# A feed-forward bias that enters through a 64-row matmul instead of a GpSimd addition

## The chip, the cores and the metric

The kernel runs on one NeuronCore of a Trainium2 chip. The time is that of one execution on the device, in microseconds (us); several executions are made and their median is what counts. The engines are called by the names of the profile: PE is TensorE (PEld its weight loads), DVE is VectorE, ACT is ScalarE, POOL is GpSimd and SP is SyncE.

## The reference

`x` has 4 sequences of 1024 tokens with 256 features (float32), `ctx` 154 tokens for each sequence. One block of gated cross attention and one gated feed-forward layer:

```
x = x + tanh(g_xattn) * attention(layernorm(x), ctx, mask, ...)   # 4 query heads of 64, one key/value head
h = gelu(layernorm(x) @ ternary(W1).T + b1)                       # 256 -> 1024
x = x + tanh(g_ffn) * (h @ ternary(W2).T + b2)                    # 1024 -> 256
```

`ternary(w)` replaces each weight by -1, 0 or 1 (round of `w` over its mean magnitude, clipped). The bias of the change is `b2`, a vector of 256 numbers that is added to every token's output.

## The kernel before, in words

The 4096 tokens are worked on as 8 groups (`NG = 8`) of 512 tokens, each group as 4 tiles (`NT = 4`) of 128 tokens. Every engine runs its own list of instructions, in an order that is written out by hand in a function `step(i, p, b)`; `i` is the number of the step, and one step does work of three groups: the attention of group `i`, the first feed-forward product, gelu and split (`ffn_in`, `gelu`, `split_h`) of group `i-1`, and the second feed-forward product `ffn_out` of group `i-2`. Steps 0 and 1 are written out, steps 2 to 5 come from a loop of two steps each, steps 6 and 7 and the two last ones (8 and 9, that have no attention) are written out again. Engines wait for each other through semaphores alone.

PE multiplies in float32r. Where the precision asks for it an operand is split into a high part (`_hi`, written by ACT as float32r) and the rest (`_lo`, written by DVE by subtraction), and both parts are multiplied. So `ffn_out(t)` (L1103) is 8 chunks times 2 parts = 16 matmuls of 128 contraction rows and 256 columns that add up in one PSUM bank. PSUM banks `ps_m` are two, taken in turn by `q1, q2, y0, q3, y1, y2, y3, att0, ...` (`M_ORDER`, L221); before a bank is written again, `bank_m` (L1008) waits until DVE has read what was in it two uses ago. DVE's `ffn_out(t)` (L785) takes the bank, multiplies by the gate and adds to the tile of `x1` (L796). `x1` holds the output of the attention part; its layer norm (`x1n`, ACT L519) is taken before anything else is added to it.

The bias: in the set-up DVE makes `b2_gated = tanh(g_ffn) * b2` (L725) in all 128 partitions. In each step from 1 to 8 POOL adds it to the four tiles of `x1` in one instruction (`add_b2`, L384 to L391) between its `normalise(0)` and `normalise(1)` (L402 to L408, that divide the softmax by its sum). It waits for `x1n_done`, so that the layer norm has read `x1` first, and DVE waits for `y_base` ahead of each L796.

In step order PE does (L1163 on): `q_T(0)`, `q(1)`, `q(2)`, `scores(0)`, `ffn_out(0)`, `q_T(1)`, `q(3)`, `ffn_out(1)`, `q_T(2)`, `x1_T(0)`, `scores(1)`, `ffn_out(2)`, `q_T(3)`, `x1_T(1)`, `scores(2)`, `ffn_out(3)`, `scores(3)`, `p_T(0)`, `tail_T(0)`, `ffn_in(0)`, `ffn_in(1)`, `p_T(1)`, and so on. `p_T` and the other transposes write `ps_t`, whose two banks come free when DVE has done its `lo_part` (L650). `products` (L925 to L929) is the helper in which most matmuls are recorded, as L928. In step 9 PE does the rest of `last_out` (L1123): its 16 matmuls for each tile are L1133, and two of the tiles start within step 8, between the pieces of `ffn_in`.

Of the kernel before, what the change touches and what calls it, by code (L numbers as in the profile page):

```python
# [7 lines left out]
F32 = mybir.dt.float32  # L8
F32R = mybir.dt.float32r
U8 = mybir.dt.uint8  # L10
ALU = mybir.AluOpType
# [17 lines left out]
def flamingo_block(nc, x, ctx_main, ctx_tail, mask, gates, rms_scale, wq, wk, wv, wo, w1t, b1, w2t, b2,  # L29
# [10 lines left out]
    NF = F // P  # L40
    TAIL = S - P
    TP = 32
    HP = H // 2
    CT = B + 1
    assert H * TP == P and B * TP == P and 2 * C == P and NG == 2 * B and KD == 2
# [4 lines left out]
    with ExitStack() as ctx:  # L50
# [26 lines left out]
        w_scale = sb("w_scale", [P, 2])  # L77
        w_thr = sb("w_thr", [P, 2, 2])
        b1_sb = sb("b1_sb", [P, NF])
        b2_gated = sb("b2_gated", [P, D])  # L80
        mask_u8 = sb("mask_u8", [P, B, S], U8)
        mask_bias = sb("mask_bias", [P, B, S])
        mask_now = sb("mask_now", [P, S])
# [85 lines left out]
        def psum(name):  # L169
# [9 lines left out]
        x_in = [sem("x_in0"), sem("x_in1")]  # L179
        out_done, last_out_done = [sem("out_done0"), sem("out_done1")], [sem("last_out_done0"), sem("last_out_done1")]  # L180

        const_set, ctx_zeroed, zeros_set, gate_set = (
            sem(n) for n in ("const_set", "ctx_zeroed", "zeros_set", "gate_set"))
        ctx_bn_done, ctx_stats, ctx_ms_done, ctx_rstd, ctx_normed, ctxT_filled, ctxT_copied = (
            sem(n) for n in ("ctx_bn_done", "ctx_stats", "ctx_ms_done", "ctx_rstd", "ctx_normed",
                             "ctxT_filled", "ctxT_copied"))
# [17 lines left out]
            sem(n) for n in ("bn1_done", "ln1_stats", "ln1_var", "ln1_rstd"))  # L204
        bn2_done, ln2_stats, ln2_var, ln2_rstd, ln2_shift, x1n_done = (
            sem(n) for n in ("bn2_done", "ln2_stats", "ln2_var", "ln2_rstd", "ln2_shift", "x1n_done"))
        q_roped, exp_done, inv_done, prob_done, y_base = (
            sem(n) for n in ("q_roped", "exp_done", "inv_done", "prob_done", "y_base"))


        def has(i):
# [129 lines left out]
        @block.gpsimd  # L341
        def _(pool):
            pool.memset(ctx_sb[:, B, :], 0.0).then_inc(ctx_zeroed, 1)
            pool.memset(neghalf[:], -0.5).then_inc(const_set, 1)
            pool.memset(ones_sb[:], 1.0).then_inc(const_set, 1)
            pool.dma_start(gate_raw[:, :], gates.partition_broadcast(P)).then_inc(gate_in, 16)
            pool.dma_start(mask_u8[:], mask.partition_broadcast(P)).then_inc(mask_in, 16)
            pool.dma_start(b2_raw, b2.partition_broadcast(P)).then_inc(b2_in, 16)

            pool.memset(prob_tail[:], 0.0).then_inc(zeros_set, 1)  # L350
            pool.memset(kk_hi[:].bitcast(F32), 0.0).then_inc(zeros_set, 1)
            pool.memset(kk_lo[:].bitcast(F32), 0.0).then_inc(zeros_set, 1)
            pool.memset(v_tail.bitcast(F32), 0.0).then_inc(zeros_set, 1)

            pool.wait_ge(ctx_stats, 1)
            pool.tensor_tensor(ctx_m2[:], ctx_mv[:, :, 0], ctx_mv[:, :, 0], ALU.mult).then_inc(ctx_ms_done, 1)
            pool.wait_ge(ctx_ms_done, 1)
            pool.tensor_tensor(ctx_ms[:], ctx_m2[:], ctx_mv[:, :, 1], ALU.add).then_inc(ctx_ms_done, 1)
            pool.wait_ge(ctx_ms_done, 2)
            pool.tensor_scalar(ctx_me[:], ctx_ms[:], RMS_EPS, None, ALU.add).then_inc(ctx_ms_done, 1)  # L360
            pool.wait_ge(ctx_ms_done, 3)
            pool.wait_ge(const_set, 1)
            pool.tensor_tensor(ctx_r[:], ctx_me[:], neghalf[:, 0:CT], ALU.pow).then_inc(ctx_rstd, 1)

            def rstd(ve, r, var_sem, rstd_sem, i):
                pool.wait_ge(var_sem, i + 1)
                pool.tensor_tensor(r[:], ve[:], neghalf[:, 0:NT], ALU.pow).then_inc(rstd_sem, 1)

            rstd(ve1, r1, ln1_var, ln1_rstd, 0)

            pool.wait_ge(wo_hi_set, 1)
            pool.tensor_tensor(wo_lo[:], wo_raw[:], wo_hi[:], ALU.subtract).then_inc(wo_set, 1)
            def rope_add(i, t):
                pool.wait_ge(m_read, m_use(i, f"q{t}") + 1)
                q = q_cos[t % 2][:].rearrange("p (h j c) -> p h j c", h=H, j=2)
                swapped = q_sin[t % 2][:].rearrange("p (h j c) -> p h j c", h=H, j=2)[:, :, ::-1, :]
                pool.tensor_tensor(q, q, swapped, ALU.add).then_inc(q_roped, 1)  # L377

            def step(i, p, b):
                att, nxt, f1, _ = has(i)  # L380

                first = isinstance(i, int) and i == 0

                def add_b2():  # L384

                    if f1:
                        pool.wait_ge(x1n_done, i * NT)
                        if isinstance(i, int) and i == 1:
                            pool.wait_ge(b2_set, 1)
                        b2s = b2_gated[:].rearrange("p (a d) -> p a d", a=1).to_broadcast([P, NT, D])  # L390
                        pool.tensor_tensor(x1[1 - p], x1[1 - p], b2s, ALU.add).then_inc(y_base, 1)  # L391

                def rstd2():
                    if f1:
                        rstd(ve2, r2, ln2_var, ln2_rstd, i - 1)

                if not att:
                    rstd2()
                    add_b2()
                    return  # L400

                def normalise(t):  # L402
                    pool.wait_ge(inv_done, i * NT + (t + 1))
                    inv = p_inv[:, t, :].rearrange("p (h a) -> p h a", a=1)
                    main, tail = prob[t][:, :, 0:P], prob[t][:, :, P:S]
                    pool.tensor_tensor(main, main, inv.to_broadcast([P, H, P]), ALU.mult)  # L406
                    pool.tensor_tensor(prob_tail[:, t, :, 0:TAIL], tail, inv.to_broadcast([P, H, TAIL]),
                                       ALU.mult).then_inc(prob_done, 1)  # L408

                rope_add(i, 1)  # L410
                rstd2()
                rope_add(i, 2)
                rope_add(i, 3)
                normalise(0)
                add_b2()
                normalise(1)
                if first:
                    w_low_piece(0)
                normalise(2)
                if first:  # L420
                    w_low_piece(1)
                if nxt:
                    rstd(ve1, r1, ln1_var, ln1_rstd, i + 1)
                normalise(3)
                if first:
                    for n in range(2, 2 * PIECES):
                        w_low_piece(n)
                if nxt:
                    rope_add(i + 1, 0)

            rope_add(0, 0)

            pool.wait_ge(v_set, 2)
            pool.wait_ge(zeros_set, 4)
            for h in range(H):
                pool.tensor_copy(v_tail[:, :, h, TP * h:TP * (h + 1)],
                                 v_T[:, B * P:].rearrange("p (b j) -> p b j", b=B)).then_inc(v_tail_set, 1)

            def w_low_piece(n):

                m, cols = n // PIECES, slice(n % PIECES * PIECE, (n % PIECES + 1) * PIECE)
                if n == 0:
                    pool.wait_ge(w_thr_set, 2)
                if n >= NL:
                    pool.wait_ge(w_set, n - NL + 1)
                pool.tensor_scalar(w_low[n % NL], w_raw[m][:, cols], w_thr[:, 1, m:m + 1], None,  # L446
                                   ALU.is_lt).then_inc(w_low_set, 1)

            loop(pool, step)
# [169 lines left out]
        def _(dve):  # L619
# [102 lines left out]
            dve.tensor_scalar(mask_bias[:], mask_u8[:], MASK_FILL, -MASK_FILL, ALU.mult, ALU.add).then_inc(mask_f_set, 1)  # L722
            dve.wait_ge(gate_set, 1)
            dve.wait_ge(b2_in, 16)
            dve.tensor_scalar(b2_gated[:], b2_raw, gate[:, 1:2], None, ALU.mult).then_inc(b2_set, 1)  # L725
            dve.wait_ge(mask_f_set, 1)

            def vw_lo_part(n):

# [22 lines left out]
            def step(i, p, b):  # L752
# [32 lines left out]
                def ffn_out(t):  # L785
# [3 lines left out]

                    n = m_use(i, f"y{t}")  # L790
                    dve.wait_ge(m_filled, n + 1)
                    dve.wait_ge(y_base, i - 1)
                    ys = x1[p][:, t, :]
                    last = isinstance(i, int) and i > NG
                    src = last_bank(t) if last else m_bank(i, f"y{t}")
# [128 lines left out]
        def _(pe):  # L924
# [83 lines left out]
            def bank_m(i, what):  # L1008
# [2 lines left out]
                    pe.wait_ge(m_read, n - 1)  # L1011
                return m_bank(i, what)[:, 0:D]

            def q(i, t):
                tile = slice(P * t, P * (t + 1))
                products(bank_m(i, f"q{t}"), [(a[:, k, tile], w[:, k, :]) for k in range(KD)
# [3 lines left out]
            def step(i, p, b):  # L1020
# [82 lines left out]
                def ffn_out(t):  # L1103
# [2 lines left out]
                        return  # L1106
                    w = w_tern[1][:].rearrange("p (c d) -> p c d", c=NF)
                    dst = bank_m(i, f"y{t}")
                    for c in range(NF):
                        if t == 0 and c in (0, NF - 2):  # L1110
                            pe.wait_ge(h_split, (i - 1) * NF - (2 if c == 0 else 0))
                        for a in (hT_hi, hT_lo):
                            m = pe.matmul(dst, a[:, c, P * t:P * (t + 1)], w[:, c, :],  # L1113
                                          start=(c == 0 and a is hT_hi), stop=(c == NF - 1 and a is hT_lo))
                    m.then_inc(m_filled, 1)

                def x_T(k):
# [5 lines left out]
                def last_out(t, chunks):  # L1123

                    w = w_tern[1][:].rearrange("p (c d) -> p c d", c=NF)
                    for c in chunks:
                        if c == 0 and t < 2:
                            dst = bank_m(NG + 1, f"y{t}")
                        else:
                            dst = last_bank(t)[:, 0:D]  # L1130
                        pe.wait_ge(h_split, (NG - 1) * NF + c + 1)
                        for a in (hT_hi, hT_lo):
                            m = pe.matmul(dst, a[:, c, P * t:P * (t + 1)], w[:, c, :],  # L1133
                                          start=(c == 0 and a is hT_hi), stop=(c == NF - 1 and a is hT_lo))
                        if c == NF - 1:
                            m.then_inc(m_filled, 1)

# [129 lines left out]
```

## Time and profile before

| | |
|---|---|
| median of 3 runs | 347.42 us (346.23 to 348.87) |
| the profiled execution | 346.31 us, of which the span from first to last instruction is 344.4 us |
| matmuls | 2175, PE busy 91% of the span |
| DVE, ACT, POOL busy | 74%, 68%, 37% |
| mean granted TensorE clock | 0.97 of 2.4 GHz, 1.00 between 117 and 289 us |
| one step of the loop, from a start of `ffn_out(1)` on PE to the next (151.10 to 185.98) | 34.9 us |
| L391, the addition on POOL | 8 times, 2.4 us each |

Busy shares are means over the whole span. A matmul's time in the profile runs from its start to the modelled end of its results, so in a full pipeline the next one starts well before: what a matmul takes of the engine is the distance between two starts.

### The profile page before, as it was taken

To read this page: it belongs to the slowest core of one execution; us is meant where nothing else is said; L and a number is where in the kernel's file an instruction comes from. 1 tells how busy PE (TensorE), PEld (TensorE's weight loads), DVE (VectorE), ACT (ScalarE), POOL (GpSimd) and SP (SyncE) were. 2 spreads that over 40 slices of the span, in tenths; PEclk is the share of its full clock that TensorE was granted. 3 is DMA by queue.
4 is the path that set the end of the run, shared out by engine and by line. 5 is a ranking of instruction groups with operands and counts; after the bars stand their busy time and mean duration, and the time that the engine had idled before them with its cause. 6 is when DMAs were issued, how large, how long until landed. Compare 5 with 4: busy or idle time off the path is not lost.

```text
span 344.4 us, 6831 instructions
## 1 busy us (share of the span) xinstructions
PE 311.7 (91%) x2175; PEld 285.4 (83%) x2175; DVE 256.4 (74%) x825; ACT 232.5 (68%) x595; POOL 127.0 (37%) x151
## 2 busy tenths in 40 slices
PE   8299649766699999999999999999999999999996
PEld 8297539655599988998899988998899889988976
DVE  0567884998559986988698869986998697858443
ACT  0144793337597579757975797579758985896492
POOL 8231237954510363036303540353136313630300
PEclk9769998998799999999999999999999999999999
DMA  6943000020000110011002100110011000100101
GB/s 127 284 129 122 2 0 2 0 64 1 0 2 0 64 47 17 0 63 48 17 0 61 46 15 0 61 46 15 0 64 46 18 0 2 47 17 2 46 16 63
DMA packets 12983, 13.35 MB, mean 39 GB/s; under 512 B 1781, under 2 KB 12397, under 8 KB 12957
## 3 DMA queue, kind: packets, MB, share of 16 engines
q1 hardware_dynamic: 11004, 11.52, 10.4%
q10 hardware_dynamic: 1824, 1.30, 1.5%
q0 software_dynamic: 128, 0.21, 0.8%
q8 instruction: 14, 0.23, 0.3%
q14 instruction: 13, 0.10, 0.1%
HBM read 8.83 MB, written 4.19 MB: 38 GB/s over the span
## 4 chain that ended last, share of the span: by engine, by line
PE 64%; DVE 21%; issue 4%; POOL 4%; ACT 3%; DMA 2%; SPq 0%; DVEq 0%; POOLq 0%
PE ps_m L928 18%; PE ps_h L928 17%; PE ps_m L1113 10%; PE ps_s L928 5%; PE ps_t L936 4%; PE ps_t L1062 3%; DVE s_neg L765 3%; DMA w_raw<-in_ctx_tail 2%; POOL hT_lo L446 2%; DVE s_neg L763 2%; DVE q_sin L708 2%; DVE s_min L769 1%; DVE q_cos L705 1%; DVE x1nT_lo L650 1%; DVE pT_lo L650 1%
## 5 line engine op out<-in xcount | busy, mean ns | idle before, releaser
L406 POOL TENSOR_TENSOR prob<-prob,p_inv 128x512 f32<-128x512 f32 x32 | 33.4, 1044 | 72.4 <-DVE p_inv L773 72.4
L377 POOL TENSOR_TENSOR q_cos<-q_cos,q_sin 128x256 f32<-128x256 f32 x32 | 23.5, 735 | 97.6 <-DVE q_sin L708 97.6
L928 PE MATMUL ps_h<-x1nT_hi,w_tern 128*128 128x512 f32 x128 | 55.0, 429 | 3.1 <-DVE vw_lo L732 2.6
L526 ACT ACTIVATE prob<-s_neg,s_min 128x154 f32<-128x154 f32 x128 | 52.5, 414 | 5.8 <-DVE s_min L769 4.9
L1113 PE MATMUL ps_m<-w_tern,hT_hi 128*128 128x256 f32 x224 | 55.3, 285 | 0.7 <-DVE x_both L796 0.2
L1113 PE MATMUL ps_m<-w_tern,hT_lo 128*128 128x256 f32 x224 | 54.7, 282 | 0.0
L928 PE MATMUL ps_h<-x1nT_lo,w_tern 128*128 128x512 f32 x128 | 51.3, 401 | 0.0
L824 DVE TENSOR_TENSOR hT_lo<-h_all,hT_hi 128x512 fp32r<-128x512 f32 x64 | 42.0, 691 | 8.8 <-ACT hT_hi L557 8.8
L557 ACT ACTIVATE h_all<-ps_h,b_sb 128x512 f32<-128x512 f32 x64 | 45.6, 712 | 3.2 <-PE ps_h L928 2.2
L928 PE MATMUL ps_m<-vw_hi,pT_hi 128*128 128x256 f32 (+1 forms) x160 | 46.7, 292 | 0.0
L557 ACT ACTIVATE hT_hi<-ps_h,b_sb 128x512 fp32r<-128x512 f32 x64 | 45.7, 714 | 0.0
L928 PE MATMUL ps_m<-vw_hi,pT_lo 128*128 128x256 f32 (+1 forms) x160 | 45.2, 283 | 0.0
L928 PE MATMUL ps_m<-vw_lo,pT_hi 128*128 128x256 f32 (+1 forms) x160 | 45.2, 282 | 0.0
L1113 PEld LDWEIGHTS ps_m<-w_tern,hT_hi 128*128 128x128 f32 x224 | 42.6, 190 | 1.9 <-DVE x_both L796 1.9
L476 ACT ACTIVATE qT_hi<-ps_t 128x256 fp32r<-128x256 f32 x32 | 12.2, 382 | 46.1 <-PE ps_t L1037 46.1
L1113 PEld LDWEIGHTS ps_m<-w_tern,hT_lo 128*128 128x128 f32 x224 | 42.7, 191 | 0.0
L650 DVE TENSOR_TENSOR pT_lo<-ps_t,pT_hi 128x512 fp32r<-128x512 f32 x64 | 29.4, 481 | 17.5 <-ACT pT_hi L476 16.9
L928 PEld LDWEIGHTS ps_h<-x1nT_hi,w_tern 128*128 128x128 f32 x128 | 24.6, 192 | 11.3 <-ACT hT_hi L557 4.6
L476 ACT ACTIVATE pT_hi<-ps_t 128x512 fp32r<-128x512 f32 x64 | 27.2, 451 | 8.6 <-PE ps_t L1062 8.5
L928 PEld LDWEIGHTS ps_m<-vw_lo,pT_hi 128*128 128x128 f32 x160 | 30.6, 191 | 0.3
L928 PEld LDWEIGHTS ps_m<-vw_hi,pT_hi 128*128 128x128 f32 x160 | 30.5, 191 | 0.4
L928 PEld LDWEIGHTS ps_m<-vw_hi,pT_lo 128*128 128x128 f32 x160 | 30.6, 191 | 0.0
(136 smaller groups left out, 802.4 us busy)
## 6 DMA issues: line engine op xcount, KB each, us to landing
x_sb<-in_x SPq DMA_DIRECT2D x8, 512.0 KB, 3.6
out_x<-x_both SPq DMA_DIRECT2D x8, 384.0 KB, 2.5
h_all<-in_w1t SPq DMA_DIRECT2D x1, 1024.0 KB, 13.7
w_raw<-in_w2t SPq DMA_DIRECT2D x1, 1024.0 KB, 5.4
out_x<-x_both SPq DMA_DIRECT2D x8, 128.0 KB, 1.7
w_raw<-in_ctx_main SPq DMA_DIRECT2D x1, 512.0 KB
wo_raw<-in_wo ACTq DMA_DIRECT2D x2, 256.0 KB, 10.2
x_both<-in_wq ACTq DMA_DIRECT2D x1, 256.0 KB, 10.7
```

The source lines that it names most:

```text
L377: pool.tensor_tensor(q, q, swapped, ALU.add).then_inc(q_roped, 1)
L406: pool.tensor_tensor(main, main, inv.to_broadcast([P, H, P]), ALU.mult)
L476: nc.scalar.activation(dst, src, ACT.Copy).then_inc(t_hi, 1)
L526: e = nc.scalar.activation(prob[t][:, h, :], s_neg[t % 2][:, h, :], ACT.Exp, bias=s_min[t % 2][:, h:h + 1], scale=-1.0, accum_out=p_sum[:, ...
L557: g = nc.scalar.activation(dst, ps_h[c % 2][:], ACT.Gelu, bias=b1_sb[:, c:c + 1])
L650: dve.tensor_tensor(dst, src, hi, ALU.subtract).then_inc(t_lo, 1)
L765: dve.tensor_tensor_reduce(s[:, h, :], ps_s[h // 2][:, S * (h % 2):S * (h % 2 + 1)], mask_now[:], 1.0, 3.4e38, ALU.add, ALU.min, least[:, ...
L824: dve.tensor_tensor(hT_lo[:, c, :], h_act[c % 4][:], hT_hi[:, c, :], ALU.subtract).then_inc(h_split, 1)
L928: m = pe.matmul(dst, lhs, rhs, start=(n == 0), stop=(n == len(pairs) - 1))
L936: m = pe.transpose(dst[:, P * t:P * (t + 1)], src[:, t, P * k:P * (k + 1)], ident_sb[:])
L1062: m = pe.transpose(t_bank(i, f"p{t}")[:, P * h:P * (h + 1)], prob[t][:, h, 0:P], ident_sb[:])
L1113: m = pe.matmul(dst, a[:, c, P * t:P * (t + 1)], w[:, c, :], start=(c == 0 and a is hT_hi), stop=(c == NF - 1 and a is hT_lo))
```

## The change

The bias enters as the first matmul of each output tile. A tile `b2_rows` holds, in partitions 0 to 31, `b2` rounded to float32r and, in partitions 32 to 63, what the rounding lost; `mean_rows` is filled with 1/32. One matmul of 64 contraction rows (`start_with_b2`) then puts `b2` into each row of the PSUM bank, and the 16 products add to it. The gate is applied by DVE's L796, as for the products. POOL's `add_b2`, its semaphore `y_base` and DVE's wait for that go; POOL sets `mean_rows` at the start; DVE's one multiplication L725 becomes a copy, a wait for the copy, and a subtraction over 32 partitions.

```diff
-        b2_gated = sb("b2_gated", [P, D])
+        b2_rows = sb("b2_rows", [P, D], F32R)
+        mean_rows = sb("mean_rows", [P, P], F32R)
...
+            pool.memset(mean_rows[:].bitcast(F32), 1.0 / ROWS).then_inc(mean_set, 1)
             pool.memset(prob_tail[:], 0.0).then_inc(zeros_set, 1)
...
-                def add_b2():
-
-                    if f1:
-                        pool.wait_ge(x1n_done, i * NT)
-                        if isinstance(i, int) and i == 1:
-                            pool.wait_ge(b2_set, 1)
-                        b2s = b2_gated[:].rearrange("p (a d) -> p a d", a=1).to_broadcast([P, NT, D])
-                        pool.tensor_tensor(x1[1 - p], x1[1 - p], b2s, ALU.add).then_inc(y_base, 1)
...
                 if not att:
                     rstd2()
-                    add_b2()
                     return
...
                 normalise(0)
-                add_b2()
                 normalise(1)
...
             dve.wait_ge(b2_in, 16)
-            dve.tensor_scalar(b2_gated[:], b2_raw, gate[:, 1:2], None, ALU.mult).then_inc(b2_set, 1)
+            dve.tensor_copy(b2_rows[:], b2_raw).then_inc(b2_hi_set, 1)
             dve.wait_ge(mask_f_set, 1)
+            dve.wait_ge(b2_hi_set, 1)
+            dve.tensor_tensor(b2_rows[ROWS:2 * ROWS], b2_raw[ROWS:2 * ROWS], b2_rows[ROWS:2 * ROWS],
+                              ALU.subtract).then_inc(b2_set, 1)
...
                     dve.wait_ge(m_filled, n + 1)
-                    dve.wait_ge(y_base, i - 1)
...
+            def start_with_b2(dst):
+
+                pe.matmul(dst, mean_rows[0:2 * ROWS, :], b2_rows[0:2 * ROWS, :], start=True, stop=False)
...
                     dst = bank_m(i, f"y{t}")
+                    if isinstance(i, int) and i == 2 and t == 0:
+                        pe.wait_ge(mean_set, 1)
+                        pe.wait_ge(b2_set, 1)
+                    start_with_b2(dst)
                     for c in range(NF):
...
                             m = pe.matmul(dst, a[:, c, P * t:P * (t + 1)], w[:, c, :],
-                                          start=(c == 0 and a is hT_hi), stop=(c == NF - 1 and a is hT_lo))
+                                          start=False, stop=(c == NF - 1 and a is hT_lo))
...
+                        if c == 0:
+                            start_with_b2(dst)
                         pe.wait_ge(h_split, (NG - 1) * NF + c + 1)
```

## Rows read from the trace of the kernel before

**Rows 1.** The page's busy times and shares of the span

```profile
PE 311.7 (91%) x2175; PEld 285.4 (83%) x2175; DVE 256.4 (74%) x825; ACT 232.5 (68%) x595; POOL 127.0 (37%) x151
```

**Rows 2.** L391 alone: ns min/median/max; the list of waiters is empty

```profile
L391 POOL TENSOR_TENSOR x_both<-x_both,b_gated x8: 2381/2415/2422, 84.7 to 322.4; 128x1024 f32<-128x1024 f32 x8
...
who waited for it (us, times):
```

**Rows 3.** The chain in order of time, one step: start us, us, what

```profile
151.10 2.18 PE ps_m L1113 x16
...
154.78 1.92 PE ps_m L1113 x16
...
158.25 0.32 DVE s_neg L763
...
160.92 0.76 issue
...
163.64 0.66 PE ps_t L1062 x4
```

**Rows 4.** Timeline of PE, its idle time and the last matmuls ahead of it

```profile
150.76 0.28 PE L928 MATMUL ps_m<-wq_hi,xT_lo 128*128 128x256 f32 x1
151.10 0.39 PE L1113 MATMUL ps_m<-w_tern,hT_hi 128*128 128x256 f32 x1
151.32 0.28 PE L1113 MATMUL ps_m<-w_tern,hT_lo 128*128 128x256 f32 x1
...
163.00 0.40 PE L928 MATMUL ps_h<-x1nT_lo,w_tern 128*128 128x512 f32 x1
163.64 0.66 PE L1062 MATMUL ps_t<-ident_sb,prob 128*128 128x128 f32 x4 [0.25 <-DVE pT_lo L650]
```

**Rows 5.** Timeline of POOL and DVE around one L391

```profile
158.33 2.42 POOL L391 TENSOR_TENSOR x_both<-x_both,b_gated 128x1024 f32<-128x1024 f32 x1
160.69 1.06 POOL L406 TENSOR_TENSOR prob<-prob,p_inv 128x512 f32<-128x512 f32 x1
...
156.76 0.17 DVE L773 RECIPROCAL p_inv<-p_sum 128x4 f32<-128x4 f32 x1
157.01 1.04 POOL L406 TENSOR_TENSOR prob<-prob,p_inv 128x512 f32<-128x512 f32 x1 [2.73 <-DVE p_inv L773]
...
160.41 0.17 DVE L773 RECIPROCAL p_inv<-p_sum 128x4 f32<-128x4 f32 x1
160.87 0.90 DVE L641 TENSOR_SCALAR ve<-mv 128x4 f32<-128x4 f32 x1
```

**Rows 6.** The chain at the end of the kernel

```profile
296.90 1.91 PE ps_m L1113 x16
...
317.41 5.74 PE ps_m L1113 x48
...
324.03 1.91 PE ps_m L1113 x16
...
329.42 0.48 PE ps_m L1133 x4
...
339.53 2.17 PE ps_t L1133 x18
```

**Rows 7.** Timeline of DVE in the set-up, and the PE work behind it

```profile
34.18 0.35 DVE L725 TENSOR_SCALAR b_gated<-x_both,gate 128x256 f32<-128x256 f32 x1
34.55 0.42 DVE L650 TENSOR_TENSOR qT_lo<-ps_t,qT_hi 128x256 fp32r<-128x256 f32 x1
...
35.68 0.23 DVE L866 COPY mask_now<-mask_bias 128x154 f32<-128x154 f32 x1
...
35.03 0.41 PE L928 MATMUL ps_s<-kk_hi,qT_hi 128*128 128x308 f32 x1 [0.89 <-DVE qT_lo L650]
```

**Rows 8.** Timeline of POOL at the start

```profile
1.02 0.20 POOL L345 MEMSET ones_sb<- 128x128 f32 x1
...
12.78 0.20 POOL L356 TENSOR_TENSOR ctx_m<-ctx_mv 128x5 f32<-128x5 f32 x1 [5.17 <-DVE ctx_mv L625]
```

More of the change, by code:

```diff
@@ L42, in flamingo_block @@
     TP = 32
+    ROWS = 32
     HP = H // 2
@@ L180, in flamingo_block @@
         out_done, last_out_done = [sem("out_done0"), sem("out_done1")], [sem("last_out_done0"), sem("last_out_done1")]
-        const_set, ctx_zeroed, zeros_set, gate_set = (
-            sem(n) for n in ("const_set", "ctx_zeroed", "zeros_set", "gate_set"))
+        const_set, ctx_zeroed, zeros_set, gate_set, mean_set, b2_hi_set = (
+            sem(n) for n in ("const_set", "ctx_zeroed", "zeros_set", "gate_set", "mean_set", "b2_hi_set"))
         ctx_bn_done, ctx_stats, ctx_ms_done, ctx_rstd, ctx_normed, ctxT_filled, ctxT_copied = (
@@ L206, in flamingo_block @@
             sem(n) for n in ("bn2_done", "ln2_stats", "ln2_var", "ln2_rstd", "ln2_shift", "x1n_done"))
-        q_roped, exp_done, inv_done, prob_done, y_base = (
-            sem(n) for n in ("q_roped", "exp_done", "inv_done", "prob_done", "y_base"))
+        q_roped, exp_done, inv_done, prob_done = (
+            sem(n) for n in ("q_roped", "exp_done", "inv_done", "prob_done"))
         def has(i):
@@ L1133, in last_out @@
                             m = pe.matmul(dst, a[:, c, P * t:P * (t + 1)], w[:, c, :],
-                                          start=(c == 0 and a is hT_hi), stop=(c == NF - 1 and a is hT_lo))
+                                          start=False, stop=(c == NF - 1 and a is hT_lo))
                         if c == NF - 1:
```

## The prediction

> **What bounds the kernel now.** I read the page's busy times first [rows 1]: PE 91%, DVE 74%, POOL 37%. PE is close to full, POOL is the idlest, so the change takes work from the engine with most room and gives it to the one with least. A share is a mean, though, and what counts is which wait ends last. So the second view is the chain that ended last, in order of time, for one step of 34.9 us [rows 3]. It changes hands: from 151.10 to 158.2 PE runs without a pause (`ffn_out(1)`, `ffn_out(2)` and what lies between); from 158.25 to 163.6 it is DVE's masks and statistics; from 163.64 to 180.2 PE again; then DVE until the next 151.10. Third, the timeline of PE beside the pauses, to see how much room PE has in the two stretches that DVE sets [rows 4]. Last, the instruction to be removed and its neighbours [rows 2, 5].
>
> **What goes away on POOL.** Eight L391 of 2.42 us, 19.3 us of POOL time [rows 2]. No instruction waited for one of them: the list of waiters under that row is empty. The next instruction on POOL is `normalise(1)` (L406), and it does start where the addition ends, at 160.69 [rows 5], so it looks held back. But what it needs, `p_inv` of tile 1, is only made from 160.41 on, and where POOL is free L406 starts 0.25 us after the start of its reciprocal (156.76 and 157.01 in the same rows). Without the addition it would start at 160.66: 0.03 us gained. This matters on the chain, because DVE's L641 of 128x4 elements takes 0.90 us there and ends at 161.77, when POOL's L406 ends (161.75) [rows 5]: it stands still while that POOL instruction runs, and the chain shows it as 0.76 us of "issue" [rows 3]. It gets its 0.03 us back in each of the 5 steps (2 to 6) that have this pattern, 0.15 us in all, and goes on waiting. In step 1 and in the last two steps L406 is not behind an addition or nothing is left behind it: nothing. DVE's wait for `y_base` was never the last one: nothing.
>
> **What comes on PE.** 32 matmuls of 128x256, as many as there are output tiles. No row of this kernel shows 64 contraction rows: every matmul's tile is printed as `128*128`. The nearest row is L1113 itself, of the same columns and type: 16 of them take 1.92 us on the chain [rows 3], so 0.12 us each. Fewer rows save nothing that I can read out of a row, so 0.12 is the lower bound. The upper bound comes from what a pipeline costs that is emptied and filled again: in a full pipeline a matmul starts 0.12 us after the one before, while its results end 0.28 us after its start, so waiting for them costs 0.16; and after a pause the second matmul comes 0.22 us behind the first and not 0.12 [rows 4], 0.10 more. Emptied before and after each bias matmul that is 0.12 + 2 x 0.26 = 0.64 us. I take 0.12, since the row with the same shape is nearer than a guess about rows, and keep 0.64 for the range.
>
> Now where they lie. In steps 2 to 6:
> - y0: `ffn_out(1)` waits until DVE has read y0, and starts at 151.10, while the matmul before it, of 256 columns, started at 150.76 and would have let it start at 150.88 [rows 4]. PE has 0.22 us of room, and 0.12 disappears in it.
> - y1 and y2: both in the stretch where PE sets the pace [rows 3]. 0.12 each. The bank for y1 is only free when DVE has read y0, so its bias matmul can't start before the wait ends.
> - y3: behind it PE comes to `ffn_in(1)`, whose last matmul starts at 163.00 and takes 0.23 us of the engine, and then waits until 163.64 for DVE [rows 4]. 0.41 us of room, 0.12 disappears. The cover is DVE's stretch; were that shorter by more than 0.3 us, these 0.12 would count too.
>
> So 0.24 us in each of 5 steps, 1.20 us. In step 7 the chain stays on PE from y1 to y3 (at 296.90 y3 stands on it) [rows 6]: 3 x 0.12 = 0.36. In step 8 all four tiles are on it, three of them at 317.41 and one at 324.03: 0.48. At the end `last_out` is on it, from its first pieces at 329.42 to its last tile at 339.53 [rows 6]: 4 x 0.12 = 0.48. Together 2.52 us, 21 of the 32 matmuls.
>
> **The set-up.** On DVE the multiplication L725 (0.35 us, the next instruction starts 0.37 after it) lies on the path to the first scores, which PE starts at 35.03 after 0.89 us of waiting for the `qT_lo` behind it [rows 7]. In its place: a copy, a wait for it, and a subtraction. A copy of 154 elements takes 0.23 us and a subtraction of 256 elements 0.42, its successor starting some 0.07 before its end [rows 7]. The copy can't be under 0.23 and with 256 elements hardly over 0.35; with the wait between them the two come to 0.6 to 0.75, so 0.25 to 0.4 more than now. I take 0.3, all of it on the path, since what follows (ACT's sums, POOL's `w_low_piece`) is a chain without a gap. POOL's `mean_rows` is a set of 128x128 elements, 0.20 us [rows 8], in front of a pause of 5.17 us before L356: nothing. The two new waits of PE at step 2 are for things done 80 us before: nothing. No DMA is added or moved.
>
> **The sum.** 2.52 + 0.3 - 0.15 = 2.7 us. The profiled execution took 346.31 us (span 344.4, 1.9 around it), so its like would take 349.0. The median of the three runs, 347.42, is 1.1 us above that execution, and I put the same 2.7 us on it: 350.1 us, 0.8% more.
>
> **Rivals.**
> 1. *The pipeline is emptied at each change between 128 and 64 rows.* The mechanism: the results of the matmul before must be out before the array works with another number of rows, and the weights behind can't be loaded ahead. It decides as soon as the price of a bias matmul is over 0.17 us. In PE's stretches the whole price counts; y1 starts after a pause, so only the way out counts there (0.12 + 0.26); y0 and y3 have rooms of 0.22 and 0.41 us. At 0.64 a step pays 0.38 + 0.64 + 0.3 + 0.15, about 1.5 us, and 5 steps 7.4; step 7 pays 2.0, steps 8 and 9 8 x 0.64 = 5.1; with the set-up 14.7 us, 362. At half the extra, 0.38 us: 5 x 0.63 + 1.0 + 3.0 + 0.15 = 7.4, so 355. Against it: the stretch from 151.10 has transposes between its products, a change of another kind, and the chain goes through it on PE alone [rows 3]; for it: none of that work changes the number of rows. The time would be slower than before by over 1%. The Trainium skill, page "TensorEngine Tiling (Array Packing)", section Key Properties, states that changing the tiling mode, and not just the tile, drains TensorE, and lists 64x128 as a mode of its own beside 128x128; no row here shows such a change, and by this rule the time would be that of this rival.
> 2. *POOL's freedom frees DVE.* If L641 came ahead of L406, or if the addition slowed DVE or ACT from beside it, the 0.76 us of standing still would go in 5 steps: 3.8 us less, so -1.1 us in all, 346.3. Against: L406 would start 0.25 us after the reciprocal starts and L641 0.46 after it [rows 5], so POOL is first by 0.2 us with or without the addition; and the mask that DVE makes at 158.25, when L391 begins beside it, takes 0.32 us [rows 3], with nothing in it to give back. The Trainium skill, page "Advanced Engine Details and Errata", section Mode Summary, says that the second SBUF port of VectorE is shared with GpSimd and that the two block each other; the 0.90 us of L641 agree, and they also show that the blocker is L406 and not L391.
> 3. *The whole is hidden.* If DVE set the pace in the 151 to 158 us stretch too, only the last steps would pay: 348.9. Against: the chain holds to PE there, and comes to DVE only when `scores(2)` are done, at 158.25 [rows 3].
>
> **How the numbers follow.** This case as summed: 0.45; rival 1: 0.42; rival 2: 0.08; rival 3: 0.05. The likeliest gives 350.1, with 349.3 to 351.2 as its own range (the set-up between 0.2 and 0.5, a price between 0.11 and 0.15, 0.3 us of scatter of a median). The range that should hold 8 times in 10 has to reach far into rival 1: 348.3 to 360.5. About 1% (3.5 us) is what a measurement of this kernel can tell from no change. The forecast's own case lies near that line, with 0.3 of its 0.45 within 1%; rival 1 is slower throughout; rivals 2 and 3 lie within 1% for the most part. So faster 0.04, within 1% 0.42, slower 0.54.
>
> **What would show it.** In the changed kernel's profile: the new matmuls as a group of 32, with the distance from one's start to the next matmul's start (0.12 for me, up to 0.38 on each side for rival 1), and above all whether the tile is printed as `64*128`; a step of 35.1 us in place of 34.9; L641 still 0.9 us long in the place where it is 0.90; POOL starting L406 0.25 us after the reciprocal; and `qT_lo` in the set-up 0.3 us later. I am wrong if PE shows pauses beside the new matmuls, or if L641 is short.

## The result, and the profile after

Four runs of the changed kernel have a median of 358.42 us (357.70 to 358.95), beside 346.85 us for the kernel before: 1.032 times as long, 95% interval 1.027 to 1.037. The change costs 11.6 us where 2.7 were forecast. The likeliest case of the prediction did not happen; rival 1 did, at a price between its two worked figures.

The page of the changed kernel, busy times and the chain by engine:

```profile
PE 328.7 (92%) x2207; PEld 295.0 (83%) x2207; DVE 258.3 (72%) x826; ACT 231.9 (65%) x595; POOL 108.3 (30%) x144
...
PE 82%; DVE 7%; POOL 4%; ACT 3%; DMA 2%; issue 1%; SPq 0%; DVEq 0%; POOLq 0%
```

The same line of the kernel before:

```profile
PE 64%; DVE 21%; issue 4%; POOL 4%; ACT 3%; DMA 2%; SPq 0%; DVEq 0%; POOLq 0%
```

PE has 32 matmuls and 17.0 us of busy time more than in [rows 1], POOL 18.7 us less. The chain, that was 64% PE, is 82% PE: in the loop's steps the waits for DVE that gave PE room have gone. The 32 matmuls, by their durations in ns (minimum/median/maximum):

```profile
L1010 PE MATMUL ps_m<-b_rows,mean_rows x30: 379/381/384, 114.8 to 340.7; 64*128 64x256 f32 x30
L1010 PE MATMUL ps_t<-b_rows,mean_rows x2: 381/381/381, 348.4 to 351.8; 64*128 64x256 f32 x2
```

The tile is printed as `64*128`, where every matmul of the kernel before had `128*128`. What that does stands in the timeline of PE around y1 and around y2 of step 4, against [rows 4]:

```profile
189.65 0.28 PE L922 MATMUL ps_m<-wq_hi,xT_lo 128*128 128x256 f32 x1
189.86 0.38 PE L1010 MATMUL ps_m<-b_rows,mean_rows 64*128 64x256 f32 x1
190.17 0.39 PE L1115 MATMUL ps_m<-w_tern,hT_hi 128*128 128x256 f32 x1
190.40 0.28 PE L1115 MATMUL ps_m<-w_tern,hT_lo 128*128 128x256 f32 x1
...
193.56 0.30 PE L922 MATMUL ps_s<-kk_hi,qT_lo 128*128 x1
193.79 0.38 PE L1010 MATMUL ps_m<-b_rows,mean_rows 64*128 64x256 f32 x1
194.10 0.39 PE L1115 MATMUL ps_m<-w_tern,hT_hi 128*128 128x256 f32 x1
```

Read the distances between starts. On the way in, 0.21 us behind a matmul of 256 columns that takes 0.12 in a row: 0.09 more. The bias matmul holds the engine for 0.31 us in place of 0.12: 0.19 more. The first L1115 takes 0.39 us, as the first L1113 after a pause in [rows 4], and the second comes 0.23 behind it in place of 0.12: 0.11 more. That is 0.39 us on top of 0.12, and no other engine is named as the releaser of a wait in it. The chain says the same for one tile: 0.31 + 2.11 us, where 16 products took 1.92 in [rows 3].

```profile
189.93 0.31 PE ps_m L1010
190.24 2.11 PE ps_m L1115 x16
...
193.86 0.31 PE ps_m L1010
194.17 2.11 PE ps_m L1115 x16
...
197.80 0.31 PE ps_m L1010
198.11 2.11 PE ps_m L1115 x16
200.22 0.85 PE ps_s L922 x6
```

The chain now stays on PE from y1 to the attention; the stretch that belonged to DVE in [rows 3] is gone. A step, from the start of y1's products in step 2 to the same in step 7, divided by 5, was 34.67 us ((289.83 - 116.47) / 5) and is 35.77 us ((297.40 - 118.53) / 5). The 12.6 us between the two spans (344.4 and 357.0) fall into three parts at these points: 2.1 us ahead of y1 of step 2, 5.5 in the five steps, 5.0 from step 7 to the end, which is what ten bias matmuls of 0.50 make. The first part holds the longer set-up on DVE:

```profile
32.63 0.28 DVE L717 CAST b_rows<-x_both 128x256 fp32r<-128x256 f32 x1
33.02 0.41 DVE L720 TENSOR_TENSOR b_rows<-x_both,b_rows 32x256 fp32r<-32x256 f32 x1
33.46 0.42 DVE L642 TENSOR_TENSOR qT_lo<-ps_t,qT_hi 128x256 fp32r<-128x256 f32 x1
```

From the start of the copy to `qT_lo` it is 0.83 us, against 0.37 in [rows 7]: 0.46 more. That it shows in the time can't be read from the profiles: `qT_lo` starts at 33.46 here and at 34.55 in the profile before, so all that came ahead of it was shorter, and from there to y1 of step 2 it is 3.2 us longer. In that stretch lie y0's bias matmul and a lower granted clock from 44 to 60 us, to which I come at the end; no run separates the two.

### The profile page after: what moved, and what is told of

Same layout as the page of the kernel before. It is cut to its first block, busy times and chain, and to the rows that moved or that the text cites. A ratio compares the mean times of both kernels' runs of the same rounds, so it can differ in the third digit from the quotient of the medians.

```text
span 357.0 us, 6849 instructions
## 1 busy us (share of the span) xinstructions
PE 328.7 (92%) x2207; PEld 295.0 (83%) x2207; DVE 258.3 (72%) x826; ACT 231.9 (65%) x595; POOL 108.3 (30%) x144
## 4 chain that ended last, share of the span: by engine, by line
PE 82%; DVE 7%; POOL 4%; ACT 3%; DMA 2%; issue 1%; SPq 0%; DVEq 0%; POOLq 0%
PE ps_m L922 21%; PE ps_h L922 19%; PE ps_m L1115 17%; PE ps_s L922 8%; PE ps_t L930 4%; PE ps_t L1060 4%; PE ps_m L1010 3%; DMA w_raw<-in_ctx_tail 2%; POOL hT_lo L438 2%; PE ps_t L1035 2%; PE ps_t L1137 1%; PE ps_m L1137 1%; DVE vw_lo L727 1%; ACT hT_lo L498 1%; PE ps_t L1067 1%
## 5 line engine op out<-in xcount | busy, mean ns | idle before, releaser
L1115 PE MATMUL ps_m<-w_tern,hT_hi 128*128 128x256 f32 x224 | 57.6, 296 | 0.0
L1115 PE MATMUL ps_m<-w_tern,hT_lo 128*128 128x256 f32 x224 | 54.7, 282 | 0.0
L1115 PEld LDWEIGHTS ps_m<-w_tern,hT_hi 128*128 128x128 f32 x224 | 42.6, 190 | 3.6
L1115 PEld LDWEIGHTS ps_m<-w_tern,hT_lo 128*128 128x128 f32 x224 | 42.8, 191 | 0.0
## 6 DMA issues: line engine op xcount, KB each, us to landing
x_both<-in_wq ACTq DMA_DIRECT2D x1, 256.0 KB, 12.6
```

What stands on the lines that cost most here:

```text
L1115: m = pe.matmul(dst, a[:, c, P * t:P * (t + 1)], w[:, c, :], start=False, stop=(c == NF - 1 and a is hT_lo))
```

## The experiments

Ratios are to runs of the kernel before made on the same chip. "Step" is worked out for each kernel as above, from two starts on its chain.

| kernel | y1 of step 2, of step 7 | step | time, ratio (95%) |
|---|---|---|---|
| before | 116.47, 289.83 | 34.67 | |
| changed | 118.53, 297.40 | 35.77 | 358.42, 1.032 (1.027 to 1.037) |
| e1, 128 rows | 118.61, 292.99 | 34.88 | 350.28, 1.013 (1.010 to 1.016) |
| e2, twice | 119.17, 300.33 | 36.23 | 363.35, 1.049 (1.045 to 1.053) |
| e7, 32 rows | 118.75, 297.53 | 35.76 | 358.86, one run |
| e3, no bias matmul | 118.85, 292.04 | 34.64 | 347.20, 1.002 (1.000 to 1.005) |
| e4, no POOL addition | 118.02, 291.20 | 34.64 | 347.63, 1.004 (1.001 to 1.007) |
| e8, y1 and y2 only | 118.11, 295.29 | 35.44 | 354.22, one run |
| e9, y0 and y3 only | 119.44, 293.24 | 34.76 | 351.98, one run |
| e5, reordered | 115.51, 289.09 | 34.72 | 347.00, 1.003 (1.000 to 1.005) |
| e6, 128 rows, reordered | 119.75, 292.07 | 34.46 | 346.67, 1.001 (0.999 to 1.004) |
| e10, addition in the gap | 117.57, 287.99 | 34.08 | 342.41, 0.989 (0.986 to 0.992) |
| e11, DVE's move alone | 114.81, 285.25 | 34.09 | 343.16, 0.992 (0.988 to 0.995) |

### Is it the change of the tile? (e1, e2, e7)

```diff
-    ROWS = 32
+    ROWS = 64
```

> The changed kernel with ROWS = 64, so that the bias matmul has 128 contraction rows (64 with the rounded bias, 64 with the rest, mean 1/64) and the tile of the array never changes. Theory (the cost is the change between a 128*128 and a 64*128 tile, 0.38 us on top of 0.12 for each bias matmul): the new matmuls have a distance of 0.12 us to the next one, L1115's first is 0.28 us long again, and the time is that of the blind sum, some 2.7 us over the kernel before, ratio 1.005 to 1.012. Rival (any matmul put at the head of a tile costs 0.5 us, whatever its rows, for its weights or its operands): the time stays at 358, ratio 1.03.

The same matmul in the same place, with 128 rows:

```profile
191.65 0.31 PE L922 MATMUL ps_s<-kk_hi,qT_lo 128*128 x1
191.79 0.28 PE L1010 MATMUL ps_m<-b_rows,mean_rows 128*128 128x256 f32 x1
191.90 0.28 PE L1115 MATMUL ps_m<-w_tern,hT_hi 128*128 128x256 f32 x1
192.02 0.28 PE L1115 MATMUL ps_m<-w_tern,hT_lo 128*128 128x256 f32 x1
```

0.14 us in, 0.11 out, 0.12 to the next: nothing is lost. Of the 11.6 us, 4.2 are left (350.28 against 346.04 for the kernel before beside it): some 7 are gone with one number of the source. The step is 34.88 us, 0.24 over the kernels without bias matmuls (e3 and e4, below) and just the 2 x 0.12 of the prediction. The total is 1.013, a little above the expected 1.012; the step is as summed, so the excess lies outside the five steps. The first 118 us of e1 have the longer set-up and a lower granted clock than the kernel before (0.58 and 0.50 from 44 to 52 us, in place of 1.00), and I can't separate them.

```diff
-            pool.memset(mean_rows[:].bitcast(F32), 1.0 / ROWS).then_inc(mean_set, 1)
+            pool.memset(mean_rows[:].bitcast(F32), 0.5 / ROWS).then_inc(mean_set, 1)
...
                 pe.matmul(dst, mean_rows[0:2 * ROWS, :], b2_rows[0:2 * ROWS, :], start=True, stop=False)
+                pe.matmul(dst, mean_rows[0:2 * ROWS, :], b2_rows[0:2 * ROWS, :], start=False, stop=False)
```

> The changed kernel with the 64-row matmul made twice in a row, each with a mean of 1/64, which gives the same bias. Theory (the way into and out of the 64-row tile costs, not the matmul): the second costs its 0.12 us only, 32 x 0.12 = 3.8 us more than the changed kernel, 362, ratio 1.043. Rival (a 64-row matmul is slow by itself, 0.5 us each): 32 x 0.5 = 16 us more, 374, ratio 1.08.

```profile
187.65 0.30 PE L922 MATMUL ps_s<-kk_hi,qT_lo 128*128 x1
187.87 0.38 PE L1010 MATMUL ps_m<-b_rows,mean_rows 64*128 64x256 f32 x1
188.09 0.28 PE L1011 MATMUL ps_m<-b_rows,mean_rows 64*128 64x256 f32 x1
188.30 0.39 PE L1116 MATMUL ps_m<-w_tern,hT_hi 128*128 128x256 f32 x1
188.52 0.28 PE L1116 MATMUL ps_m<-w_tern,hT_lo 128*128 128x256 f32 x1
```

The second 64-row matmul has the ordinary 0.28 us. From the first one to the second L1116 it is 0.65 us, where the changed kernel has 0.54 (189.86 to 190.40): 0.11 us for a matmul more. Four a step make 0.46 (36.23 - 35.77). So a 64-row matmul is not slow by itself; going to it and coming back is. The total is 1.049, a little above the 1.043 that I expected and far from the 1.08 of the rival.

```diff
-                pe.matmul(dst, mean_rows[0:2 * ROWS, :], b2_rows[0:2 * ROWS, :], start=True, stop=False)
+                pe.matmul(dst, mean_rows[0:ROWS, :], b2_rows[0:ROWS, :], start=True, stop=False)
```

> The changed kernel with a bias matmul of 32 contraction rows; the part of b2 that float32r rounds off is left out. Theory (any number of rows that changes the tile costs the same change): the tile is printed 32*128, the distance to the next matmul is 0.31 us as with 64 rows, and a step stays at 35.8 us. Rival (the price goes with the rows): a distance of 0.2 us or less, or of more than 0.4.

```profile
186.43 0.30 PE L922 MATMUL ps_s<-kk_hi,qT_lo 128*128 x1
186.66 0.38 PE L1010 MATMUL ps_m<-b_rows,mean_rows 32*128 32x256 f32 x1
186.97 0.39 PE L1115 MATMUL ps_m<-w_tern,hT_hi 128*128 128x256 f32 x1
187.19 0.28 PE L1115 MATMUL ps_m<-w_tern,hT_lo 128*128 128x256 f32 x1
```

The distances are those of 64 rows, 0.23, 0.31 and 0.22, and the step is 35.76: between 64 and 32 rows the price is the same.

### What was POOL's addition worth? (e3, e4)

```diff
# e3, the changed kernel
-                    start_with_b2(dst)
-                        if c == 0:
-                            start_with_b2(dst)
-                                          start=False, stop=(c == NF - 1 and a is hT_lo))
+                                          start=(c == 0 and a is hT_hi), stop=(c == NF - 1 and a is hT_lo))
# e4, the kernel before
-                        pool.tensor_tensor(x1[1 - p], x1[1 - p], b2s, ALU.add).then_inc(y_base, 1)
+                        pass
-                    dve.wait_ge(y_base, i - 1)
```

> The changed kernel without the 32 bias matmuls, its set-up kept; nothing adds b2, so that part of the result is left out. Theory (POOL's addition cost nothing but 0.03 us a step): the kernel before plus 0.3 us for the set-up, ratio 0.998 to 1.003, and DVE's small TENSOR_SCALAR before the last mask of a step still takes 0.8 to 0.9 us. Rival (POOL's freedom frees DVE): 3.8 us less, ratio 0.989.

> The kernel before without POOL's addition and without DVE's wait for it; nothing adds b2, so that part of the result is left out. Theory: 0.15 us less than before, ratio 0.997 to 1.002. Rival (POOL's freedom frees DVE): ratio 0.989. The difference to the run before it is the set-up alone: 0.3 us in DVE's time, and the clock of the set-up if the set-up's order has a part in it.

Both have a step of 34.64 us, 0.03 under the kernel before, which is the figure of the prediction. The trace of e3 shows why it is so little:

```profile
197.60 0.17 DVE L768 RECIPROCAL p_inv<-p_sum 128x4 f32<-128x4 f32 x1
198.07 0.84 DVE L633 TENSOR_SCALAR ve<-mv 128x4 f32<-128x4 f32 x1
...
197.84 1.04 POOL L399 TENSOR_TENSOR prob<-prob,p_inv 128x512 f32<-128x512 f32 x1 [2.28 <-DVE p_inv L768]
```

POOL had been idle for 2.28 us and starts its division 0.24 us after the reciprocal, and the small instruction (L641 in [rows 5]) still stands until the division ends. Rival 2 is out: taking the addition away doesn't free DVE. The total of e4 is 1.004 and not 0.999, outside what I expected. It isn't in the steps; its first 118 us are 1.6 us longer than in the profile of the kernel before, with a granted clock of 0.59 and 0.50 from 44 to 52 us (below). What made its runs longer as a group I didn't find out.

### Where does PE have room? (e8, e9)

```diff
# e8; e9 has (0, 3)
-                    start_with_b2(dst)
+                    if t in (1, 2):
+                        start_with_b2(dst)
...
-                        if c == 0:
+                        if c == 0 and t in (1, 2):
```

> The changed kernel with the 64-row bias matmul for tiles 1 and 2 of each group alone; tiles 0 and 3 get no b2, so that part of the result is left out. To be read: the length of a step, from one first L1115 of a tile to the same one a step on, over steps 2 to 7 (before 34.67 us, without bias matmuls 34.64, changed kernel 35.77). Theory (PE has room ahead of y1 and behind y3, none around y1 and y2): y1 comes after a pause and pays only 0.32, y2 pays 0.50, so 35.46. Rival (the price is the same for all four tiles, 1.13 / 4 each): 35.2.

> The same with the bias matmul for tiles 0 and 3 alone; tiles 1 and 2 get no b2. Theory: y0's 0.50 us less PE's room of 0.22 and less the 0.10 that a start after a pause costs anyway, so 0.18; y3's 0.50 less a room of 0.41 and the same 0.10, so 0; a step of 34.8. Rival (same price for all): 35.2.

Measured: 35.44 and 34.76, against 34.64 with none. y1 and y2 cost 0.80 us of each step, y0 and y3 with the same two matmuls 0.12. The rooms ahead of y1 and behind y3, read out of [rows 4], are real. Together the four cost 1.13, more than 0.80 + 0.12. The steps say why: y0 and y3, at 2 x 0.50 us, cost 0.12 and so used up 0.88 us of PE's waiting; after that no pause is left ahead of y1, and y1 and y2 pay their whole 2 x 0.50, which with the 0.12 makes 1.12.

### Can DVE's standing still be taken away? (e5, e6, e10, e11)

Rival 2 was wrong in its cause, but it had a prize: the 0.76 us of standing still in each step. In all four kernels DVE does `variances1` ahead of `inverse(1)`; its wait for `bn1_done` moves ahead of `x1n_lo(1)`.

```diff
# DVE, all four
+                    dve.wait_ge(bn1_done, i * NT + 2 * NT)
                 x1n_lo(1)
-                    dve.wait_ge(bn1_done, i * NT + 2 * NT)
+                    variances1(i + 1)
                 inverse(1)
-                    variances1(i + 1)
# POOL: e11 leaves add_b2 in its place; e5 has it behind normalise(3), e10 ahead of it
                     rstd(ve1, r1, ln1_var, ln1_rstd, i + 1)
+                add_b2()    # e10
                 normalise(3)
+                add_b2()    # e5
```

> The kernel before with two moves and nothing of the change: DVE takes the next group's variances (L641 among them) ahead of the reciprocal for tile 1, so that POOL's division of tile 1 isn't running yet; and POOL's addition of b2 goes behind its division of tile 3, where POOL has 4.8 us free, so that it isn't running either. Theory (L641 stands still because of POOL's instruction): L641 takes 0.17 us or less there instead of 0.90, and each step gets shorter by PE's room at that place, 0.3 to 0.4 us, five times, and by up to 0.7 us in steps 0 and 1: 1.5 to 3.4 us less, ratio 0.990 to 0.996. Rival (L641 is slow by itself, or waits for its inputs): no change, ratio 0.999 to 1.002.

e5 did to L641 what was expected and nothing to the time:

```profile
L641 DVE TENSOR_SCALAR ve<-mv x16: 169/170/525, 17.2 to 319.0; 128x4 f32<-128x4 f32 x16
L824 DVE TENSOR_TENSOR hT_lo<-h_all,hT_hi x64: 675/684/1915, 98.0 to 338.0; 128x512 fp32r<-128x512 f32 x64
...
170.28 2.84 POOL L391 TENSOR_TENSOR x_both<-x_both,b_gated 128x1024 f32<-128x1024 f32 x1
...
172.06 2.22 DVE L824 TENSOR_TENSOR hT_lo<-h_all,hT_hi 128x512 fp32r<-128x512 f32 x2
```

L641's longest is 0.53 us, its median 0.17 (in the kernel before 0.91 and 0.52). But two L824, that take 1.28 us together elsewhere, take 2.22 beside POOL's addition, which itself takes 2.84 in place of 2.42 [rows 5]. The standing still had moved, with the addition, to an instruction on the chain (two pieces of L824, at 172.06 and 173.60). Neither theory that I wrote down had this; the next two kernels test it.

> The 128-row bias matmul of the earlier run with DVE's move alone (POOL has no addition there). Theory: against that run, which was 1.013 of the kernel before, L641's stand goes, but PE has 0.12 us less room behind y3: 0.2 to 0.3 us a step and up to 0.7 in steps 0 and 1, so 1.005 to 1.009. Rival: 1.013.

e6 has no addition on POOL, so nothing to meet. Its step is 34.46 us against 34.88 of e1, 0.42 less where 0.2 to 0.3 were expected, and the time falls from 1.013 to 1.001, below the expected range.

> The reordered kernel before (DVE's variances ahead of the reciprocal of tile 1), with POOL's addition put not behind its division of tile 3 but ahead of it, behind the reciprocal root for the next group, where POOL has 5 us free and DVE works on PSUM and not on two SBUF operands. Theory (a DVE instruction with two SBUF operands stands still beside POOL's, which gave back in the first reordered kernel what L641 had gained): L824 is never over 0.75 us inside the loop, L641 0.17 us, a step of 34.2 to 34.4 us in place of 34.67, ratio 0.993 to 0.996. Rival (the step is bound elsewhere, by ACT's gelu): the step stays at 34.7, ratio 1.000.

> The kernel before with DVE's move alone, POOL's addition where it was. Theory: the addition ends some 0.1 us ahead of L641, so L641 is short (0.17 to 0.3 us) and the division of tile 1, that now comes later, finds POOL free; a step of 34.2 to 34.4 us, ratio 0.993 to 0.996. Rival (L641 now stands on the addition instead of the division, since the two instructions on POOL follow each other): L641 0.5 us or more and a step of 34.6 us.

POOL's row in e10, and POOL and DVE around L641 in e11:

```profile
165.28 2.38 POOL L391 TENSOR_TENSOR x_both<-x_both,b_gated 128x1024 f32<-128x1024 f32 x1
170.36 1.04 POOL L406 TENSOR_TENSOR prob<-prob,p_inv 128x512 f32<-128x512 f32 x1 [2.69 <-DVE p_inv L773]
```

```profile
156.11 2.42 POOL L391 TENSOR_TENSOR x_both<-x_both,b_gated 128x1024 f32<-128x1024 f32 x1
158.91 1.04 POOL L406 TENSOR_TENSOR prob<-prob,p_inv 128x512 f32<-128x512 f32 x1 [0.39 <-DVE p_inv L773]
...
158.59 0.17 DVE L641 TENSOR_SCALAR ve<-mv 128x4 f32<-128x4 f32 x1
```

In e10 the addition is back at 2.38 us, and L824's longest is 0.98 us as in the kernel before. Beside this addition DVE has two L650, of 0.89 us together, and then waits 2.33 us for ACT. In e11 the addition ends at 158.53 and L641 starts at 158.59, by luck of 0.06 us. Both have a step of 34.08 or 34.09 us, 0.6 less than before, more than the 0.3 to 0.4 that I expected, and both are faster than either kernel, by 1.1% and 0.8% with intervals that overlap. I had read PE's room behind y3 (0.41 us) as the most that a shorter DVE stretch could give. In e11 just that room goes: L1062 starts 0.22 us behind the last `ffn_in(1)` matmul, in place of 0.64 in [rows 4].

```profile
160.78 0.39 PE L928 MATMUL ps_h<-x1nT_lo,w_tern 128*128 128x512 f32 x1
161.00 0.60 PE L1062 MATMUL ps_t<-ident_sb,prob 128*128 128x128 f32 x4
```

That is 0.42 us. Most of the rest lies in the eight `ps_h` matmuls further on.

```profile
168.82 2.00 PE ps_h L928 x8
166.12 1.86 PE ps_h L928 x8
```

The first line is the chain of the kernel before, the second that of e11: 0.14 us less. With e6 at 34.46, bias matmuls of 128 rows cost about 0.4 us a step against POOL's addition even where L641 is short.

## Why the prediction was right or wrong

- *The price of a bias matmul on PE*: the step that failed. The prediction took 0.12 us, "since the row with the same shape is nearer than a guess about rows". That row had the same columns and type, but not the same tile, and the tile was the one thing that the change brought in. Measured: 0.50 us. With 128 rows (e1) the same matmul takes 0.12. Of the 8.9 us between the forecast and the result this term makes some 8.3: 5 x (1.10 - 0.21) in the five steps and 10 x 0.38 behind them.
- *Rival 1*, given 0.42: right in its mechanism as far as runs can show it. It costs to change between 128 and 64 rows (e1), once for the way in and out and not for each matmul (e2), and the same for 32 rows as for 64 (e7). The upper bound of 0.64 us, two emptied and refilled pipelines, was too high, since the measured extra is 0.09 + 0.19 + 0.11 and not 2 x 0.26; the other worked price, 0.38 us, was too low. (At 0.38 y0 would have paid 0.06 us a step over its room of 0.22 and the 0.10 of a restart, which the sum leaves out: 0.3 us in all.) The Trainium skill, page "TensorEngine Tiling (Array Packing)", section Key Properties, says that changing the tiling mode drains TensorE; the 0.39 us that come with the change, and stay away in e1, agree. That results are waited for inside the array is argued and not shown. Rival 1 should have had a larger chance than the summed case: no row of the kernel before had a tile change that spoke against it.
- *Where the matmuls lie*: right. Two on the path and two in PE's pauses: e1's step of 34.88 is 0.24 over 34.64, e8 and e9 came out at 35.44 and 34.76 where 35.46 and 34.8 stood. At 0.50 us the rooms of 0.22 and 0.41 no longer cover it, and in these steps the chain lies on PE.
- *The last steps*: right in number, all tiles on the path, 10 x 0.50 = 5.0 us from y1 of step 7 to the end.
- *POOL's addition*: 0.03 us a step, measured 0.03 (e3 and e4). Rival 2, given 0.08, is out in e3 and e4, and rival 3 with the steps that pay. Rival 2's sentence on the two engines leaves out a condition: the Trainium skill, page "Advanced Engine Details and Errata", section Mode Summary, speaks of VectorE's 2p instructions, and no run here shows in which mode an instruction ran.
- *The set-up*: 0.46 us in place of 0.3. The term was mis-sized by two waits: 0.11 us pass between the end of the copy (32.91) and the subtraction that depends on it (33.02), and `qT_lo` starts 0.03 us after the end of the subtraction, where I had it start 0.07 before. That it reached the time is not shown: e3, that has it, took 347.20 us and e4, that hasn't, 347.63.
- *The range* of 348.3 to 360.5 held the 358.42 only because it had to reach into rival 1; 0.54 for slower was on the right side, by rival 1 and not by the summed case, and the single number was not.

## What to carry to other kernels

Here a matmul of few rows between full ones cost what its tile cost to change, and fewer rows saved nothing: look at the tile that the profile prints, and fill up to 128 rows if the neighbours have them. POOL's addition, for which nobody waited, was worth 0.03 us a step when it was removed, and still did harm in e5, where it ran beside instructions of DVE that then took longer. Ask what runs beside such an operation; in e10 and e11 it lay where DVE worked on PSUM or waited, and in the steps shown nothing on the chain stood still beside it. When a stall that was removed leaves the time as it was, look for the same stall at the place to which the work was moved.

## What the runs showed of the hardware that was not expected

- Changing between a `128*128` tile and a `64*128` or `32*128` one costs 0.39 us for the way in and back (0.09 + 0.19 + 0.11) at the full clock; a second matmul of 64 rows behind the first costs 0.11.
- A DVE instruction of 4 elements (0.17 us alone) took up to 0.91 us beside POOL's division, and 0.17 where the order of DVE kept the two apart (e11); two subtractions of two SBUF operands took 2.22 us in place of 1.28 beside POOL's addition (e5).
- The granted clock of the set-up differs from run to run. In the profile of the kernel before it is 1.00 from 44 to 52 us and 0.67 and 0.90 in the next 8, in that of the changed kernel:

```profile
44.00:48.00 4.00, 3.02 (x13) 2.33 (x12) 2.84 (x15) 3.52 (x15) 2.32 (x4) 0.57 0.01 4
48.00:52.00 4.00, 1.88 (x9) 1.45 (x7) 2.97 (x14) 2.30 (x10) 0.00 (x0) 0.50 0.00 0
52.00:56.00 4.00, 3.91 (x16) 3.64 (x17) 1.11 (x4) 0.84 (x3) 3.68 (x4) 0.50 0.00 0
```

  (stretch, its length, busy time and count of PE, PEld, DVE, ACT and POOL, then the clock; 0.50 is the lower level, 1.2 GHz.) In the 4 us ahead of this, from 40 to 44, the clock is 1.00 in both, and PE is busy for 1.82 us in the changed kernel and for 2.47 in the kernel before. The 13 runs of the kernel before beside e10 had mean clocks of 0.960 to 0.975 and times of 347.94 to 344.41 us, so I estimate from these that 1 to 2 us of any single comparison of two profiles can be this. The lengths of steps are free of it: from 118 to 286 us the granted clock is 1.00 in every profile here.
